# A gated feed-forward block with adapters: the first tile's adapter products moved forward, the down projection's adapter steps cut into single pieces

## The reference, cut to what matters

```python
x = x + _L0_cond_ref(x, W, b, coeff, mask)          # x @ (W^T + coeff * (2*mask - 1)) + b

def lora_add(base, inp, A, B):
    t = jnp.einsum('bri,bni->bnr', A[layer_idx][lora_indices], inp)
    return base + jnp.einsum('bor,bnr->bno', B[layer_idx][lora_indices], t) * SCALE
gate = lora_add(jnp.einsum('bnh,fh->bnf', x, W_gate), x, A_gate, B_gate)
up = lora_add(jnp.einsum('bnh,fh->bnf', x, W_up), x, A_up, B_up)
act = jax.nn.silu(gate) * up
down = lora_add(jnp.einsum('bnf,hf->bnh', act, W_down), act, A_down, B_down)
return x + down
```

## Time and profile before

| | |
|---|---|
| runs, median (range) | 1599.0 us (1595.74 to 1599.19) |
| the profiled execution's own time | 1594.07 us |
| its span | 1592.4 us |
| TensorE busy | 1549.6 us, 97% |
| VectorE busy | 1221.5 us, 77% |
| ScalarE busy | 804.6 us, 51% |
| POOL (DMA issue) busy | 427.1 us, 27% |
| mean granted TensorE clock | 0.995 |
| the chain that ended last, share of the span | TensorE 86%, VectorE 8% |

### The profile page before, as it was taken

The page is one execution under the profiler, slowest core; times in us unless marked ns, Lnnn a source line. Parts: engine busy times, 40 slices in busy tenths (PEclk is TensorE's granted clock), DMA queues, the critical chain, the costliest instruction groups (busy, mean ns, idle before and its releaser), DMA issues.

```text
span 1592.4 us, 23426 instructions
## 1 busy us (share of the span) xinstructions
PE 1549.6 (97%) x7550; PEld 1305.7 (82%) x7550; DVE 1221.5 (77%) x2136; ACT 804.6 (51%) x1478; POOL 427.1 (27%) x821
## 2 busy tenths in 40 slices
PE   6999998999999999999999979999999999999999
PEld 6999976888888888878888858888888888778887
DVE  8999877766677677688888886677767666788886
ACT  8999855444444444443334464444444444433332
POOL 0000133333333333253410024322313233543100
PEclk9999999999999999999999999999999999999999
DMA  9999853444444444698593625444444445996653
GB/s 373 373 365 368 300 176 114 145 151 146 144 144 156 155 156 155 231 358 268 174 374 111 238 70 174 138 140 139 155 144 149 136 155 181 340 340 208 223 195 118
DMA packets 141962, 325.66 MB, mean 205 GB/s; under 512 B 22417, under 2 KB 50321, under 8 KB 141841
## 3 DMA queue, kind: packets, MB, share of 16 engines
q0 software_dynamic: 61216, 176.21, 32.9%
q1 hardware_dynamic: 76016, 139.57, 25.9%
q10 hardware_dynamic: 4608, 8.39, 1.4%
HBM read 233.51 MB, written 90.18 MB: 203 GB/s over the span
## 4 chain that ended last, share of the span: by engine, by line
PE 86%; DVE 8%; issue 2%; ACT 2%; DMA 1%; SPq 1%; POOL 0%; DVEq 0%; POOLq 0%; ACTq 0%
PE ps L1474 58%; PE ps L1470 25%; PE ps L1612 3%; DVE m_raw L1110 1%; DVE m_lo L1107 1%; DVE acc L1110 1%; DVE lo L1107 1%; DVE op_b L1107 1%; DMA m_raw<-in_mask 1%; DVE raw L1107 1%; DVE fx L1107 0%; DMA b_in<-in_b_gu 0%; DMA x_scratch<-x_out 0%; SPq L504 0%; POOL b_in L644 0%
## 5 line engine op out<-in xcount | busy, mean ns | idle before, releaser
L1474 PE MATMUL ps<-op_b,hi 128*128 128x512 f32 x1616 | 501.6, 392 | 7.1 <-ACT p5c L779 3.7
L1107 DVE TENSOR_TENSOR lo<-raw,hi 128x512 fp32r<-128x512 f32 (+2 forms) x640 | 333.8, 531 | 132.7 <-ACT hi L779 130.7
L779 ACT ACTIVATE hi<-raw 128x512 fp32r<-128x512 f32 (+1 forms) x592 | 305.7, 520 | 222.3 <-PE ps L1474 185.5
L1474 PEld LDWEIGHTS ps<-op_b,hi 128*128 128x128 f32 x1616 | 305.2, 189 | 71.8 <-ACT p5c L779 4.7
L1474 PE MATMUL ps<-op_b,lo 128*128 128x512 f32 x808 | 317.0, 392 | 0.0
L1474 PE MATMUL ps<-op_d,hi 128*128 128x512 f32 x800 | 248.6, 392 | 8.5 <-DVE acc L1110 8.3
L1470 PE MATMUL ps<-op_b,hi 128*128 128x512 f32 x816 | 253.5, 392 | 0.0
L626 POOL DMA_DIRECT2D operand_scratch<-ot x140 | 75.3, 540 | 548.5 <-DVE ot L1107 534.6
L1110 DVE TENSOR_TENSOR acc<-acc,ps 128x512 f32<-128x512 f32 x248 | 170.0, 686 | 53.8 <-PE ps L1474 47.3
L1474 PEld LDWEIGHTS ps<-op_d,hi 128*128 128x128 f32 x800 | 147.9, 188 | 44.3 <-DVE acc L1110 13.9
L1470 PEld LDWEIGHTS ps<-op_b,hi 128*128 128x128 f32 x816 | 154.2, 189 | 31.3
(11 more groups left out here) (130 smaller groups left out, 2323.9 us busy)
## 6 DMA issues: line engine op xcount, KB each, us to landing
operand_scratch<-ot POOLq DMA_DIRECT2D x140, 512.0 KB, 3.9
op_d<-operand_scratch POOLq DMA_DIRECT2D x140, 512.0 KB, 10.6
raw<-in_wgu SPq DMA_DIRECT2D x168, 256.0 KB, 3.9
m_raw<-in_mask SPq DMA_DIRECT2D x64, 512.0 KB, 5.4
raw<-in_wd SPq DMA_DIRECT2D x160, 128.0 KB, 3.8
w_in<-in_w SPq DMA_DIRECT2D x32, 512.0 KB, 6.3
x_scratch<-x_out POOLq DMA_DIRECT2D x32, 256.0 KB, 4.5
acc<-x_scratch POOLq DMA_DIRECT2D x16, 512.0 KB, 6.6
```

Of the source, the lines that this page charges most:

```text
L779: return nc.scalar.activation(o, i, ACT.Copy)
L1107: return nc.vector.tensor_tensor(o, a, b, ALU.subtract)
L1474: return mm(dst, weight, v, start=False, stop=stop, skip_group_check=True)
```

## The change

- The first tile's B rows lie in `b_w` like all others; `b_first` is gone. So the rows of tile 1 are copied to `b_w` only after r of half 1, by `lora_b(s, 1)` inside `first_result` of half 1, and p3 of tile 1, which needs them, comes behind r.
- r of half 0 stands behind row tile 3 of half 1 (before: behind row tile 5).
- r of half 1 stands behind p6 of tile 1 (before: behind p7), its result before p3's; td of tile 0 stands before p2 (before: behind it).
- Behind p1 of tile 1, the split t3 of k = 1 comes before VectorE's low parts of `t_gate` and `t_up`.
- `half_tile` comes behind the add of p5 (before: ahead of it), `half_tile_hi` behind p6 (p1), `half_tile_lo` behind p3 (p5).
- The adapter steps of the down projection are single instructions behind single products, over row pairs 1 to 3 (before: groups of 2 or 3 instructions over row pairs 1 and 2).

No instruction is added or taken away. POOL's and SP's orders stay.

```diff
-T_DOWN_AT = {(hp, u): (hp - 1, step) for hp in (1, 2)
-             for u, step in (("p5", "low"), ("p3", "sum"), ("p7", "hi"), ("p4", "ready"))}
+T_DOWN_AT = {(1, "p5"): ("low", 0), (1, "p6"): ("sum", 0, 0), (1, "p7"): ("sum", 0, 1), (1, "p4"): ("hi", 0),
+             (2, "p5"): ("ready", 0, 0), (2, "p3"): ("ready", 0, 1),
+             (2, "p2"): ("low", 1), (2, "p4"): ("sum", 1, 0), (3, "p5"): ("sum", 1, 1), (3, "p3"): ("hi", 1),
+             (3, "p2"): ("ready", 1, 0), (3, "p4"): ("ready", 1, 1)}
...
-            ("g", 1, "p1"): [("t high", 1), ("t low", 1)] + forms("t3", 1, 2) + [("lora_b", 1)] + forms("t3", 3),
-            ("r", 1): [("result", 1), ("t neg",)]}
+            ("g", 1, "p1"): [("t high", 1)] + forms("t3", 1) + [("t low", 1)] + forms("t3", 2, 3),
+            ("r", 1): [("result", 1)],
+            ("g", 1, "p3"): [("t neg",)]}
...
-            if o == KQ + 2:
+            if o == KQ:
...
-        order += [("g", s, 1, u) for u in PRODUCTS[:5]] + [("r", s, 1), ("g", s, 1, "p2"), ("td", s, 0), ("g", s, 1, "p4")]
+        order += [("g", s, 1, u) for u in PRODUCTS[:3]] + [("r", s, 1)]
+        order += [("g", s, 1, u) for u in PRODUCTS[3:5]] + [("td", s, 0)] + [("g", s, 1, u) for u in PRODUCTS[5:]]
...
                 if f > 1:
                     act.wait_ge(pe_done, done["g", s, f - 1, "p4"])
-                else:
-                    act.wait_ge(pe_done, done["h", s, 0, 0])
-                copy((b_w if f else b_first)[:, :, :], b_in[c % 2][:, :, f % 2 * P:(f % 2 + 1) * P]).then_inc(bw_h, 1)
+                elif f:
+                    act.wait_ge(pe_done, done["r", s, 1])
+                elif s:
+                    act.wait_ge(pe_done, last_left(s - 1))
+                copy(b_w[:, :, :], b_in[c % 2][:, :, f % 2 * P:(f % 2 + 1) * P]).then_inc(bw_h, 1)
...
-                if key[0] == "d" and key[2:] == (0, 0, "p1"):
+                if key[0] == "d" and key[2:] == (0, 0, "p6"):
                     half_tile_hi(key[1], 1)
...
-                if key[0] == "d" and key[2:] == (0, 0, "p1"):
+                if key[0] == "d" and key[2:] == (0, 0, "p5"):
                     half_tile(key[1], 1)
-                if key[0] == "d" and key[2:] == (0, 0, "p5"):
+                if key[0] == "d" and key[2:] == (0, 0, "p3"):
                     half_tile_lo(key[1], 1)
```

More of the change, by code:

```diff
@@ L73, in first_tile_steps @@
             ("ta", 0, 5): a_part(1, 0) + [("make", 2)] + forms("t1", 1),
-            ("ta", 0, 7): a_part(1, 2) + [("lora_b", 0), ("t sum", 0), ("make", 3)] + forms("t1", 2)
+            ("ta", 0, 7): a_part(1, 2) + [("lora_b",), ("t sum", 0), ("make", 3)] + forms("t1", 2)
                           + [("t own", 0), ("t high", 0), ("t low", 0)] + forms("t1", 3),
@@ L1088, in _ @@
                 if key[0] == "d" and key[2] == 0 and key[3:] in T_DOWN_AT:
-                    half, step = T_DOWN_AT[key[3:]]
+                    step, *args = T_DOWN_AT[key[3:]]
                     if step == "low":
-                        t_down_low(key[1], half)
+                        t_down_low(key[1], *args)
                     elif step == "hi":
-                        t_down_hi(key[1], half)
+                        t_down_hi(key[1], *args)
                 if key[0] == "d" and key[2] == SEGS - 1:
@@ L1174, in lora_b @@
                 dve.wait_ge(bw_h, s * FT + f + 1)
-                q, tile = slice(R2, 2 * R2), b_w if f else b_first
-                sub(tile[q, :, :], b_in[f // 2 % 2][q, :, f % 2 * P:(f % 2 + 1) * P], tile[q, :, :]).then_inc(bw_l, 1)
+                q = slice(R2, 2 * R2)
+                sub(b_w[q, :, :], b_in[f // 2 % 2][q, :, f % 2 * P:(f % 2 + 1) * P], b_w[q, :, :]).then_inc(bw_l, 1)
             def raw_in(g, name):
@@ L1258, in first_result, with t_down_sum, t_down_pick @@
                     operand_lo((s, 0, "t1"), t_sum[:, :])
-            def t_down_sum(s, half):
+            def t_down_sum(s, half, b):
                 n = HALVES * s + half
                 dve.wait_ge(td_low, 2 * (n + 1))
[L1263 to L1267, removed]
+                r, cols = 2 * DR * b, slice(b * S, (b + 1) * S)
+                nc.vector.scalar_tensor_tensor(
+                    out=td_w[0:DR, 1, cols], in0=ps[6 + half][r:r + DR, cols], scalar=LORA_SCALE,
+                    in1=td_w[r:r + DR, 0, cols], op0=ALU.mult, op1=ALU.add).then_inc(td_sum, 1)
+            def t_down_pick(s, half):
+                n = HALVES * s + half
                 dve.wait_ge(td_sum, 2 * (n + 1))
@@ L1270, in t_down_sum, with t_down_ready @@
                                         ).then_inc(td_pick, 1)
-            def t_down_ready(s, half):
+            def t_down_ready(s, half, i):
                 n = HALVES * s + half
@@ L1275, in t_down_ready @@
                 dve.wait_ge(td_hi, n + 1)
-                for r in (HALF, HALF + DR):
-                    nc.vector.scalar_tensor_tensor(
-                        out=act_t[r:r + DR, half * N:(half + 1) * N], in0=td_h[:, :], scalar=pick[:, 1:2],
-                        in1=td_w[0:DR, 0, :], op0=ALU.mult, op1=ALU.add).then_inc(td_ready, 1)
+                r = HALF + i * DR
+                nc.vector.scalar_tensor_tensor(
+                    out=act_t[r:r + DR, half * N:(half + 1) * N], in0=td_h[:, :], scalar=pick[:, 1:2],
+                    in1=td_w[0:DR, 0, :], op0=ALU.mult, op1=ALU.add).then_inc(td_ready, 1)
             def evict(key):
@@ L1457, in _ @@
                 if key[0] == "d" and key[2] == 0 and key[3:] in T_DOWN_AT:
-                    half, step = T_DOWN_AT[key[3:]]
+                    step, *args = T_DOWN_AT[key[3:]]
                     if step == "sum":
-                        t_down_sum(key[1], half)
+                        t_down_sum(key[1], *args)
+                    elif step == "hi":
+                        t_down_pick(key[1], *args)
                     elif step == "ready":
-                        t_down_ready(key[1], half)
+                        t_down_ready(key[1], *args)
         @block.tensor
@@ L1516, in first_lora @@
                 for row, t in enumerate((t_gate[half], t_up[half])):
-                    end = mm_on(first_bank(row, half)[:, :], b_first[:, 2 * half + row, :], t[:, :])
+                    end = mm_on(first_bank(row, half)[:, :], b_w[:, 2 * half + row, :], t[:, :])
                 end.then_inc(pe_done, 1)
@@ L1570, in gate_up @@
                     if k == KQ - 1 and loras:
-                        if f == 1 and u == "p3":
-                            pe.wait_ge(t_ready, 4 * s + 4)
                         if u in ("p3", "q2"):
```

28 lines of the change are left out of this document (14 added, 14 removed).

## The result

| us | before | after |
|---|---|---|
| median, timed side by side | 1598.25 (4 executions, 1595.74 to 1599.19) | 1586.28 (4 executions, 1585.72 to 1586.72) |
| profiled execution, its span | 1594.07, 1592.4 | 1586.49, 1584.8 |

The ratio is 0.9931 with a 95% interval of 0.9918 to 0.9945: faster, by 12.0 us in these medians. Profile against profile it is 7.6 us only. So two numbers have to be explained: 7.6 us of structure, and some 3 us by which usual executions of before are longer than the one that was read.

The account below looks back on a forecast made before the run. TensorE, busy 97% of the span, was taken to bound the kernel. Per block 0 - 2.3 - 1.2 - 2.1 + 0.3 = -5.3 us, two blocks -10.6, so 1599.0 becomes 1588.4, stated as 1588; range 1581 to 1596.

Parts of the forecast that it names:

- r of half 0: Its place two row tiles earlier: TensorE idles 2.9 us, covered by 1.9 us before the next `ta`; 0 us.
- r of half 1, p3, p7, td: First tile: td's 2.20 us wait goes, a new 1.6 us wait comes in p3; 2.3 us less a block.
- p4 of tile 1 just in time: VectorE's sum behind p7 ends at 262.43, just in time for p4 at 262.6.
- The later start of p3: First tile: the split of t3 ahead of `t_gate` and `t_up` starts p3 0.57 us later.
- The clock: Behind td's wait TensorE ran near 1.2 GHz; 1.7 us of what is regained is clock, within the 2.3.
- Rival 1: Lower clock returns behind the new waits, on p3 and p7; up to 3.4 us, 1591.5 us, chance 0.12.
- Row pair 0: Down projection: without `half_tile` ahead, the add of p5 starts 1.34 us earlier; 1.2 us less a block.
- Row pairs 1 to 3: Down projection: single adapter steps remove most of 3.06 us in four waits behind groups; 2.1 us less a block.
- rival 2: Only first tile pays; row pairs 1 to 3 give 0.6 us or nothing, `acc` or VectorE late; 1593, chance 0.12.
- The load of `acc`: POOL's loads start 2.0 us later; row tile 3 lands at 694.9, needed at 694.8; 0.3 us paid a block.
- signs of being wrong: Slow stretch over p3 and p7; VectorE waiting for `acc`'s load; TensorE waits beyond 1 us in row pairs 1 to 3.
- Rival 4: Row tile 3 of `acc` lands late, p3 of row pair 1 waits 3.8 us; +5.9 a block, 1600.2, chance 0.06.

Follow-up runs that it names:

- e10: The full change with r of half 0 put back two row tiles later, behind row tile 5 of half 1; 1586.56 us, ratio 0.9937.
- e1: The full change with the down projection of the kernel before, so the first tile's part alone; 1591.91 us, ratio 0.9969.
- e4: The full change with VectorE's piece of `b_w` ahead of a low part and two raw weight sums; 1586.97 us, ratio 0.9943.
- e8: The full change with td back behind p2; 1586.50 us, ratio 0.9935.
- e9: The full change with the low parts of `t_gate` and `t_up` back ahead of VectorE's split of t3; 1586.17 us, ratio 0.9934.
- e11: The full change with the edits of e3 and e7 together; 1583.52 us, ratio 0.9917.
- e12: The full change with the edits of e3, e7 and e9 together; 1581.32 us, ratio 0.9904.
- e3: The full change with row tile 3 of `acc` loaded as soon as the memory under it is free; 1584.26 us, ratio 0.9921.
- e7: The full change with row pair 2's two raw weight sums moved behind `a`; 1585.72 us, ratio 0.9930.
- e2: The kernel before with the change's down projection alone; 1591.85 us, ratio 0.9963.
- e5: The kernel before with only `half_tile` and its parts moved as in the change; 1595.34 us, ratio 0.9986.
- e6: The kernel before with only the down projection's adapter groups split into pieces; 1593.79 us, ratio 0.9978.

## Why the prediction was right, point by point

The forecast was 10.6 us; the two profiles differ by 7.6, the medians by 12.0, or by 11.0 with the median of before over its 49 executions, 1597.2. That the medians agree so well is partly luck, for two errors of opposite sign stand behind it: the structure gave 3 us less than summed, and before's usual execution had more to lose than the one that I read. Against the profile the forecast was 1583.5 us, and the profiled execution took 1586.49.

- *r of half 0: 0 us.* Right (e10). TensorE waited 3.91 us instead of the 2.9 that I worked out, since ScalarE's `b_in` landed some 0.6 us later in this execution; the cover took it.
- *r of half 1, p3, p7, td: 2.3 us less.* The stretch gives 441.80 - 438.38 - 1.34 = 2.08 (e1: 2.08 and 2.09). The wait in p3 was to be 1.6 and is 1.54; the wait of td went, and td runs at the full clock. "p4 of tile 1 just in time" was the step that mattered, and I did not draw its conclusion: if VectorE's list sets p4, then the wait in p3 and the place of td are free (e4, e8), and so is a low clock on p3.
- *The later start of p3, 0.57 us.* The order of the splits does cost something, but more: 0.89 us a block (e9's block 0; e11 against e12, 437.39 and 436.50).
- *The clock.* The 1.7 us behind td were right, and went. For the other stretches my reading was wrong: I wrote that each block had two, behind waits of 2.2 us or more. Block 0 has three (behind 2.29, 2.47 and 2.20 us), block 1 two, and in block 1 TensorE waited 2.66 us ahead of p3 with the full clock behind it. Rival 1 said that it could fall on p3 and p7 after the change; it did in block 0 of e3, with the change's first tile, and cost nothing there; 0.7 us in e7, where VectorE's list is shorter. In the kernel before it cost 1.5 us, in four of eight blocks, and that is where part of the gain beyond 7.6 us comes from. The Trainium skill (TensorE: Matmul & The Clock Gate, Terms) puts the cost of such a stretch at its time x (1 - K/N): an estimate of 3 x 0.5 = 1.5 us for e2's 251 to 254 alone, and the trace roughly agrees, with 1.5 to 1.6 us more in S1 for the whole stretch. Whether the path pays it is not in that estimate: on p6 it paid nothing.
- *Row pair 0: 1.2 us less.* 1.34 us (e5).
- *Row pairs 1 to 3: 2.1 us less.* 1.75 to 1.85 us where no load is in the way (e3, e6), 0.54 of wait left at p3 of segment 1 as said (0.55), none at p7 of row pair 2 (0.3 said). In the full change only 0.51 and 0.57 us of it are left, because of the next term: what rival 2 said of this part, that `acc` comes late and 0.6 us or nothing is left, came true, and its 1593 was too high because it left out row pair 0 and what before's usual executions lose beyond the profile.
- *The load of `acc`: 0.3 us more.* This term failed in size: 1.2 us a block in the profiled execution, 0.8 in the mean over twelve blocks. "VectorE waiting for `acc`'s load in row pair 1" stood among my signs of being wrong, and it came: 1.51 us, with 0.93 of TensorE and the restart behind it. The waits for `acc` stayed at 4.8 us, above the 4 that I named as a sign of being right. POOL's issue was right within 0.2 us: 687.79, with TensorE 1.6 us earlier than before, against 689.2 - 1.6. What was wrong is the landing of row tile 3: I took the 4.7 us of block 0, the shortest there is. Block 1 of the same profile has 5.5, the blocks of the other kernels 4.8 to 6.1, with and without the change, and after has 6.0. The Trainium skill (Trainium Kernel Development and Optimization, Key Constraints) has all queues' transfers share 16 engines; no run here shows what the load had to share them with when it took longer. Rival 4's way was thus the right one at about a fifth of its price: 1.2 us a block of 5.9.

Block by block: 2.08 + 1.34 + 1.75 - 1.22 = 3.95, twice 7.9, less 0.48 of later `b_in` in block 0 and with 0.15 in between: 7.6.

What stays open: of the 3.1 us by which the median of before is above its profile, the low clock on p3 (1.5 us in half of the blocks, so 1.5 an execution) and a low clock behind the 2.29 us of row pair 0 (in one of the six blocks with that wait, in e1, 1.3 us) explain a part, the landing of `b_in` (up to 1.5 us) may explain another. The shares were not measured apart, and why the clock falls now behind one wait and now behind the next was not tried.

## What to carry to other kernels

When a reordering leaves a new wait on the bounding engine, ask whether the engine that it waits for would hold it a little later anyway: here 1.5 us of wait a block cost nothing and covered the low clock besides, so removing it gave nothing, and a gain came only with VectorE's own list shortened. Price a DMA that starts nearer to its use by the longest landing that the trace has for it, not by one of them, and look first whether the memory under it is free earlier. And before one profiled execution is taken as the kernel, compare it with the spread of the others: the one read here was faster than all 49 that were timed.

## What the runs showed of the hardware

Behind one and the same wait, 2.4 to 2.5 us ahead of p6, TensorE was at the lower of its two levels at once (granted clock 0.60 to 0.64 over 245 to 248 in before and after), or at the full clock there and at 0.50 on the product behind the next wait (e2, e4, e7). Within one execution it stood in one place in block 0 and in the other in block 1 (e3, e4, e6, e7, e11). A wait of 2.66 us had no low stretch behind it (block 1 of before, 1.00 over 946 to 949), and in the six blocks with 2.28 to 2.29 us of wait ahead of row pair 0's p3 one had it. A low stretch costs 1.5 to 1.6 us where nothing covers it.

The second of six loads of 512 KB in a row on POOL's queue landed 4.7 us (block 0 of before) to 6.1 us (block 1 of e10) from its issue, 5.5 in block 1 of before and 6.0 in both blocks of after, always in the same place of the queue. Issued alone 8 us earlier it took 7.4 to 8.9 us (e3, e11, e12).
